# Two layer normalisations of a transformer layer, applied by ScalarE with a scale and a bias per row, in place of VectorE

## What is computed

```python
def _layernorm(x, axis=-1, eps=1e-05):
    m = jnp.mean(x, axis=axis, keepdims=True)
    v = jnp.var(x, axis=axis, keepdims=True)
    return (x - m) / jnp.sqrt(v + eps)
# attention:
q = (x @ Wq).reshape(b, n, N_HEADS, HEAD_DIM)
k, v = jnp.split(ctx @ Wkv, 2, axis=-1)
q = apply_axial_rope(q, pos_map)
k = apply_axial_rope(k, ctx_pos_map)
logits = jnp.einsum('bqhd,bkhd->bhqk', q, k) * scale
w = jax.nn.softmax(logits, axis=-1)
attn = jnp.einsum('bhqk,bkhd->bqhd', w, v)
return attn.reshape(b, n, N_HEADS * HEAD_DIM) @ Wout + bout
# feed-forward:
xn = x * jax.lax.rsqrt(jnp.mean(x * x, axis=-1, keepdims=True) + eps) * norm_w
logits = jnp.einsum('btd,gd->btg', xn, Wc) / jnp.clip(temperature, 0.1)
top_vals, top_idx = jax.lax.top_k(logits, N_ACTIVE)
expr_w = jax.nn.softmax(top_vals, axis=-1)
expressed = jnp.einsum('btk,btkc->btc', expr_w, genes[top_idx])
down = jnp.tanh(jnp.einsum('btc,dc->btd', expressed, Wd))
up = jnp.einsum('btc,dc->btd', expressed, Wu)
return down * xn * up * scale
# layer:
x = x + attention(_layernorm(x), ctx_1024, fside_BxSx2_0, fside_BxSx2_0, ...)
x = x + feed_forward(_layernorm(x), ...)
```

## Time and profile before

| | |
|---|---|
| three timed runs | 526.91, 529.20, 530.35 us; median 529.20 us |
| profiled execution, first to last instruction | 527.0 us |
| PE busy | 457.6 us, 87% of the span |
| DVE busy | 416.1 us, 79% |
| ACT busy | 258.1 us, 49% |
| POOL busy | 262.2 us, 50% |

### The profile page before, as it was taken

One profiled execution on the slowest core, in us unless ns is written; L12 is line 12 of the kernel. 1 busy time (PEld: TensorE's weight loads), 2 busy tenths in 40 slices (PEclk: granted clock), 3 DMA queues, 4 the chain that ended last, 5 costly groups with the idle time before them and its releaser, 6 DMA issues. The chain is left out here.

```text
span 527.0 us, 10932 instructions
## 1 busy us (share of the span) xinstructions
PE 457.6 (87%) x3866; PEld 336.8 (64%) x3866; DVE 416.1 (79%) x644; ACT 258.1 (49%) x386; POOL 262.2 (50%) x263
## 2 busy tenths in 40 slices
PE   1727698999999999999999999999999999796734
PEld 0525465677776767676777777777677776565523
DVE  3574274989898989899998989898989897866680
ACT  2641626374737374645555463647464737243111
POOL 0453527282919292928374655647382919110111
PEclk9967699999999999999999999999999999979776
DMA  7940504141322314050505050505041321200000
GB/s 266 283 90 18 95 1 89 25 87 26 69 64 51 84 30 103 21 109 21 109 21 109 21 109 21 109 9 113 9 92 38 73 59 37 65 23 1 21 20 21
DMA packets 81754, 34.45 MB, mean 65 GB/s; under 512 B 73136, under 2 KB 75200, under 8 KB 81728
## 3 DMA queue, kind: packets, MB, share of 16 engines
q1 hardware_dynamic: 80768, 33.05, 27.1%
q10 hardware_dynamic: 960, 1.05, 0.6%
HBM read 12.86 MB, written 4.19 MB: 32 GB/s over the span
## 5 line engine op out<-in xcount | busy, mean ns | idle before, releaser
L830 DVE MAX8 top<-stage_b 128x8 f32<-128x1024 f32 x64 | 78.0, 1218 | 32.3 <-ACT stage_b L579 32.1
L396 POOL TENSOR_TENSOR rstd<-var,minus_half 128x1 f32<-128x1 f32 x16 | 8.8, 550 | 178.1 <-DVE var L804 178.1
L838 DVE MATCH_REPLACE8 stage_b<-top,stage_b 128x1024 f32<-128x1024 f32 x64 | 77.3, 1208 | 0.0
L367 POOL TENSOR_TENSOR stage_b<-stage_b,cos_t 128x512 f32<-128x512 f32 x32 | 41.2, 1288 | 37.0 <-issue 25.5
L994 PE MATMUL gene<-wcT_h,yT_h 128*128 128x512 f32 x128 | 53.9, 421 | 1.1 <-DVE yT_l L817 1.1
L994 PE MATMUL gene<-wcT_l,yT_h 128*128 128x512 f32 x128 | 51.8, 405 | 0.0
L994 PE MATMUL gene<-wcT_h,yT_l 128*128 128x512 f32 x128 | 51.6, 403 | 0.0
L1101 PE MATMUL dense<-stage_a,v_ext 128*32 128x128 f32 x1024 | 42.6, 287 | 2.8 <-ACT stage_a L552 2.1
L536 ACT ACTIVATE parts<-turned 128x1024 f16<-128x1024 f32 x32 | 33.8, 1057 | 19.1 <-POOL turned L380 19.1
L765 DVE TENSOR_REDUCE row_max<-score_a 128x8 f32<-128x1024 f32 x32 | 38.9, 1217 | 4.8 <-PE score_a L1060 4.8
L765 DVE TENSOR_REDUCE row_max<-score_b 128x8 f32<-128x1024 f32 x32 | 38.9, 1215 | 3.7 <-PE score_b L1060 3.5
(11 more groups left out here) (149 smaller groups left out, 1129.2 us busy)
## 6 DMA issues: line engine op xcount, KB each, us to landing
x_ring<-x_dram SPq DMA_DIRECT2D x16, 256.0 KB, 2.6
out_dram<-x_ring SPq DMA_DIRECT2D x16, 256.0 KB, 2.5
ctx_sb<-ctx_dram SPq DMA_DIRECT2D x16, 128.0 KB, 2.5
stage_a<-L_ffn_Wc_dram SPq DMA_DIRECT2D x1, 2048.0 KB, 10.1
stage_b<-L_xattn_Wq_dram ACTq DMA_DIRECT2D x1, 1024.0 KB, 5.9
stage_b<-L_xattn_Wkv_dram SPq DMA_DIRECT2D x1, 1024.0 KB, 9.3
stage_b<-L_xattn_Wout_dram SPq DMA_DIRECT2D x1, 1024.0 KB, 12.5
genes_sb<-L_ffn_genes_dram SPq DMA_DIRECT2D x2, 256.0 KB, 5.2
```

Of the source, the lines that this page charges most:

```text
L367: pool.tensor_tensor(halves(qk_cos), halves(qk_sb), trig(cos_t, t), ALU.mult).then_inc(s_cosm[n], 1)
L830: nc.vector.max(top[:, 8 * n:8 * n + 8], logit if n == 0 else rest).then_inc(s_top[n], 1)
L838: nc.vector.match_replace(rest, top[:, 8 * n:8 * n + 8], logit if n == 0 else rest, REMOVED).then_inc(s_rem[n], 1)
```

## The change

The two big VectorE instructions `norm1_apply` and `norm2_apply` become ScalarE activations with the function Identity, which compute x * scale + bias with a scale and a bias per row. The scale is `rstd`; the bias is -mean * rstd, for which VectorE gets a small 128x1 instruction at the old place (`norm1_shift`, `norm2_shift`). So each normalisation now passes from GpSimd to VectorE to ScalarE. On ScalarE the first stands behind `attn_hi` and ahead of `read_v`, the second behind `ctx_hi` and ahead of `y_hi`. `ln1` on GpSimd gets a wait, because `rstd1` is now read by ScalarE. The streams of PE and SP are the same as before. The diff without its empty lines, the new semaphores and the declarations of `shift1` and `shift2`:

```diff
@@ gpsimd
             def ln1(t):
                 pool.wait_ge(s_var1, t + 1)
+                if not first(t):
+                    pool.wait_ge(s_xn, t)
                 pool.tensor_tensor(rstd1[:], var1[:], minus_half[:], ALU.pow).then_inc(s_rstd1, 1)
@@ scalar
+            act.wait_ge(s_x, 16)
+            act.wait_ge(s_shift1, 1)
+            nc.scalar.activation(xn[:], slot(0), ACT.Identity, bias=shift1[:], scale=rstd1[:]).then_inc(s_xn, 1)
             act.wait_ge(s_wkv, 16)
...
+            def norm1_apply(t):
+                act.wait_ge(s_x, (t + 1) * 16)
+                act.wait_ge(s_shift1, t + 1)
+                if not first(t):
+                    act.wait_ge(s_xT, t)
+                nc.scalar.activation(xn[:], slot(t), ACT.Identity, bias=shift1[:], scale=rstd1[:]).then_inc(s_xn, 1)
+            def norm2_apply(t):
+                act.wait_ge(s_x1, t + 1)
+                act.wait_ge(s_shift2, t + 1)
+                if not first(t):
+                    act.wait_ge(s_yT, t)
+                    act.wait_ge(s_kept, t)
+                nc.scalar.activation(yn[:], slot(t), ACT.Identity, bias=shift2[:], scale=rstd2[:]).then_inc(s_yn, 1)
...
                 if t2 is not None:
                     attn_hi(t2)
+                if later(t0, 1):
+                    norm1_apply(t0)
                 if later(t1):
                     read_v(t1)
...
                     read_q(t0)
                     ctx_hi(t0)
                 if t2 is not None:
+                    norm2_apply(t2)
                     y_hi(t2)
...
             wcT_hi(3)
+            norm1_apply(1)
             duT_hi()
@@ vector
-            def norm1_apply(t):
+            def norm1_shift(t):
                 dve.wait_ge(s_rstd1, t + 1)
                 if not first(t):
-                    dve.wait_ge(s_xT, t)
-                nc.vector.tensor_scalar(xn[:], slot(t), mv1[:, 0:1], rstd1[:], ALU.subtract,
-                                        ALU.mult).then_inc(s_xn, 1)
+                    dve.wait_ge(s_xn, t)
+                nc.vector.scalar_tensor_tensor(shift1[:], mv1[:, 0:1], -1.0, rstd1[:], ALU.mult,
+                                               ALU.mult).then_inc(s_shift1, 1)
-            def norm2_apply(t):
+            def norm2_shift(t):
                 dve.wait_ge(s_norm2, t + 1)
                 if not first(t):
-                    dve.wait_ge(s_yT, t)
-                    dve.wait_ge(s_kept, t)
-                nc.vector.tensor_scalar(yn[:], slot(t), mv2[:, 0:1], rstd2[:], ALU.subtract,
-                                        ALU.mult).then_inc(s_yn, 1)
+                    dve.wait_ge(s_yn, t)
+                nc.vector.scalar_tensor_tensor(shift2[:], mv2[:, 0:1], -1.0, rstd2[:], ALU.mult,
+                                               ALU.mult).then_inc(s_shift2, 1)
...
                 if t3 is not None:
-                    norm2_apply(t3)
+                    norm2_shift(t3)
...
                 if later(t0, 1):
-                    norm1_apply(t0)
+                    norm1_shift(t0)
```

More of the change, by code:

```diff
@@ L117, in build @@
         mv1, mv2 = sb("mv1", [P, 2]), sb("mv2", [P, 2])
-        var1, rstd1 = sb("var1", [P, 1]), sb("rstd1", [P, 1])
-        var2, rstd2 = sb("var2", [P, 1]), sb("rstd2", [P, 1])
+        var1, rstd1, shift1 = sb("var1", [P, 1]), sb("rstd1", [P, 1]), sb("shift1", [P, 1])
+        var2, rstd2, shift2 = sb("var2", [P, 1]), sb("rstd2", [P, 1]), sb("shift2", [P, 1])
         top = sb("top", [P, TOP])
@@ L148, in build @@
             "bn1_done", "mv1_done", "var1_done", "rstd1_done", "xn_done"))
+        s_shift1, s_shift2 = sem("shift1_done"), sem("shift2_done")
         s_xT, s_cT = sem("xT_in_psum"), sem("cT_in_psum")
@@ L871, in _ @@
             norm1_stats(0)
-            norm1_apply(0)
+            norm1_shift(0)
             dve.wait_ge(s_wkv_h, 1)
@@ L949, in _ @@
             scale_up()
-            norm1_apply(1)
+            norm1_shift(1)
             wcT_lo(1)
```

## The result

The changed kernel takes 540.63 us in the median of four runs (540.2 to 541.2), the kernel before in the same comparison 528.06 us (526.04 to 530.35). The ratio is 1.0232 with a 95% interval of 1.0197 to 1.0266: slower by 12.6 us. The profiled execution took 540.2 us with a span of 538.3 us. The prediction said 545.8 us (538 to 552) and slower with a chance of 0.85.

A forecast was written before the change was run, and what follows sets the result against it. The prediction took PE to bound the kernel: 14 tiles x 1.22 us of `transpose_y` delay, less 0.5 us at the last tile, gives +16.6 us, 545.8 us on the 529.2 us median; range 538 to 552 us.

The forecast's parts named there:

- What bounds the kernel: In a middle tile PE is busy 27.18 of 27.64 us; whatever makes PE wait lengthens the tile, relieving another engine hardly shortens it.
- The rival in which VectorE sets the period: VectorE holds the loop; each of 14 tiles gives back 1.96 us, 27 us in all: 502 us; chance 0.09.
- the one with the clock: The new wait drops PE's granted clock, costing 3.25 us in each of 14 tiles: 591 us; chance 0.05.
- The delay of `transpose_y`: On PE, `transpose_y` starts 1.22 us later per tile, since `yn` waits behind `ctx_hi` on ScalarE; bounds 1.05 and 1.34 us.
- I take nothing off: From `transpose_y` to `scoresT`, PE's chain and the row-max transfer both move back by the full 1.22 us.
- The delay is absorbed: Rival: PE catches up before `scoresT` because its transfer wait is looser than it looks; within 1% of 529.2 us; chance 0.06.
- the bounds of the prediction's sum: Low and high per-tile delays over 14 tiles, less 0.5 us: +14.2 us (543.4) and +19.7 us (548.9).
- what was added toward the absorbed case: The 541 to 550 us range widened a little, as part of the delay may be given back: 538 to 552 us.
- The last tile: At the end, 0.15 us on DVE, 0.06 us handover and 0.77 us on ScalarE replace 1.48 us: 0.5 us less.
- The first normalisation: On ScalarE between `attn_hi` and `read_v`, covered by a 0.81 us wait for PE: costs nothing, allowing 0 to 0.1 us per tile.
- VectorE's relief: DVE's busy time falls by some 30 us, each shift taking about 0.15 us; worth nothing in time.

The follow-up runs named there:

- experiment 4: Changed kernel with both shifts computed by tensor_scalar (a pointer and a constant) instead of scalar_tensor_tensor: 538.37 us against 529.31 us, ratio 1.0173.
- experiment 7: Changed kernel with second normalisation ahead of `read_q` and `ctx_hi`, shifts as tensor_scalar, second shift ahead of `group_max(t2, 2)`: 529.54 us against 529.16 us, ratio 1.0011.
- experiment 8: Changed kernel with only the first normalisation on ScalarE, its shift as tensor_scalar, the second back on VectorE: 528.37 us against 529.16 us, ratio 0.9997.
- Experiment 2: Changed kernel with only the second normalisation on ScalarE, behind `ctx_hi`, the first back on VectorE: 541.50 us against 529.31 us, ratio 1.0221.
- Experiment 6: Changed kernel with second normalisation between `read_q` and `ctx_hi` on ScalarE, shifts as tensor_scalar: 533.12 us against 529.16 us, ratio 1.0077.
- experiment 9: Kernel before, with only `read_q` moved behind `ctx_hi` on ScalarE, both normalisations on VectorE: 541.97 us against 529.17 us, ratio 1.0245.
- experiment 1: Changed kernel with only the first normalisation on ScalarE, the second back on VectorE: 527.33 us against 529.31 us, ratio 0.9981.
- experiment 3: Changed kernel with second normalisation moved ahead of `read_q` and `ctx_hi` on ScalarE: 543.96 us against 529.31 us, ratio 1.0288.
- experiment 5: Changed kernel with second normalisation ahead of `read_q` and `ctx_hi` on ScalarE, and both shifts as tensor_scalar: 533.46 us against 529.16 us, ratio 1.0090.

## Why the prediction was right, and where it was off

**What bounds the kernel: right.** PE is the engine whose waits count, and relief for VectorE was worth nothing (experiment 4, with 18 us less work for VectorE than after; experiments 7 and 8, with 22 and 12 us less than before). The rival in which VectorE sets the period falls with them, and the one with the clock by the 1.00 in the tile's stretch.

**The delay of `transpose_y`: right in cause and nearly in size.** The prediction had 1.22 us from an activation behind `ctx_hi`, with 0.26 us from start to start and 774 ns of its own. Measured: 0.28 us, 0.81 us and a delay of 1.29 us in the mean of nine tiles. The Trainium skill ("ScalarE: Activation LUTs", What ACT_TABLE_LOAD costs), from which the prediction worked out an estimate of 799 ns, was nearer to the 0.81 us than the value that it took from rows. Experiment 2 shows that this place carries the whole loss, and experiment 7 that it is the place and not the engine.

**"I take nothing off": this step failed.** Of 1.29 us per tile PE gives back 0.37, so that the period grows by 0.92 us. By the table: 0.26 us up to `transpose_max` and 0.30 us up to `project_k` are given back, since `transpose_max` had waited for `group_max(3)` of VectorE before (the 1.21 us from 295.47 in the earlier trace rows end at 296.68, `transpose_max` starts at 296.83 in the earlier trace rows) and `project_k` for `ctx_lo` behind it in VectorE's stream (296.60 + 0.41 = 297.01, `project_k` starts at 297.15). Now `group_max(3)` ends no later than before (VectorE starts it at 300.38, 0.12 us behind `transpose_ctx`, against 0.22 us in the rows of before), and both of PE's steps find it done. The profile names no releaser for PE's wait ahead of `transpose_max` ("issue"); that it was `group_max(3)` is read from the times. The chain of waits has it 15 times before and once after, with PE's wait for the transfer of the row maxima below it, first before, then after:

```profile
PEld score_a L1067 <- issue: 9.1, 15, 1.2
PEld score_b L1078 <- DMA qT<-neg_maxT: 6.5, 10, 2.6
```

```profile
PEld score_a L1072 <- issue: 1.2, 1, 1.2
```

The prediction had looked for slack only between `y_hi` and `y_lo`. There is none there, but there is some at the end of that chain, between `neg_max_lo` and the transfer that follows it. VectorE's and SP's timelines before:

```profile
296.60 0.41 DVE L753 TENSOR_TENSOR cT_l<-dense,cT_h 128x256 fp32r<-128x256 f32 x1
...
298.73 0.27 DVE L771 SCALAR_TENSOR_TENSOR neg_maxT<-score_a,neg_maxT 32x128 f16<-32x128 f32 x1
```

```profile
297.54 0.55 SPq L307 DMA_DIRECT2D qT<-neg_maxT  x1
298.82 0.37 SPq L259 DMA_DIRECT2D x_ring<-x_dram  x1
299.31 0.55 SPq L307 DMA_DIRECT2D qT<-neg_maxT  x1
```

After:

```profile
305.02 0.27 DVE L777 SCALAR_TENSOR_TENSOR neg_maxT<-score_a,neg_maxT 32x128 f16<-32x128 f32 x1
```

```profile
303.53 0.55 SPq L288 DMA_DIRECT2D qT<-neg_maxT  x1
304.82 0.37 SPq L240 DMA_DIRECT2D x_ring<-x_dram  x1
305.31 0.55 SPq L288 DMA_DIRECT2D qT<-neg_maxT  x1
```

Before, `neg_max_lo` ends at 299.00 and the second transfer starts 0.31 us later, behind the load of the next x in SP's stream; after, the two are 0.02 us apart (305.29 and 305.31). The second transfer starts 1.77 or 1.78 us behind the first in both, and the first follows `neg_max_hi`, which reads what `transpose_max` wrote. So, counted from `transpose_ctx`, `neg_max_lo` is 1.28 us later than before, but the transfer only 0.99 us. In experiment 9 `neg_max_lo` is 0.20 us later than before, in the mean of the nine tiles, and the transfer is not.

PE gains 0.56 us up to `project_k`, more than the transfer does, and so 0.35 us go again at `scoresT`, where PE waits for that transfer: 11.3 us in 15 waits, against 6.5 us in 10. The remaining 0.16 us are given back behind `scoresT`, 0.09 of them in the stretch to the genes; by what was not traced. Experiment 6 has the same slack: of 0.79 us it gives back 0.42. To this extent the rival "The delay is absorbed" was right, and so was its reason, a wait for the transfer that is looser than it looks.

With the measured sizes the sum is 14 x (1.29 - 0.37) = 12.9 us, against 12.6 us by the medians; the prediction had 16.6 us. That the two agree so well is in part luck, since three of the 14 tiles lost only 0.50 to 0.67 us. The 540.63 us lie below the bounds of the prediction's sum (543.4 to 548.9 us), and below the 541 us to which the spread of the timed runs widened them; only what was added toward the absorbed case reaches down to them. Some 1.1 us of the distance come from the base, which the prediction took as 529.2 us and which is 528.06 us in the comparison.

**The last tile: not borne out.** The 0.5 us off for the last tile needed a shift of 0.15 us. It took 1.21 us there:

```profile
496.49 1.21 DVE L817 SCALAR_TENSOR_TENSOR shift<-mv,rstd 128x1 f32<-128x1 f32 x1 [0.66 <-POOL rstd L379]
```

Then 1.21 us, 0.06 us to hand over and the activation's 0.81 us take the place of the 1.48 us of the earlier trace rows, a loss of 0.6 us and no gain. PE bears it out: `transpose_y` of the last tile starts 2.16 us behind the start of the shift (at 498.65), where it started 1.53 us behind that of the normalisation (at 488.37). It can't be read from the spans: what lies behind the last `ctx_hi` differs between 91.64 and 96.26 us over the profiled kernels.

**The first normalisation: right.** ScalarE's timeline after:

```profile
319.23 0.60 ACT L552 ACTIVATE aT_h<-dense 128x512 fp32r<-128x512 f32 x1 [0.16 <-PE dense L1121]
319.73 0.80 ACT L559 ACTIVATE xn<-x_ring,shift,rstd 128x512 f32 x1
320.63 0.60 ACT L515 ACTIVATE v_ext<-score_b 128x512 f32<-128x512 f32 x1
```

It fills the gap of the earlier trace rows ahead of `read_v`, ends at 320.53, and PE's transposes of `xn` start at 320.86 without a wait for it. Experiments 1 and 8 put its price at nothing.

**VectorE's relief: mis-sized, without effect on the time.** Some 30 us less were expected, 6.4 us less came, chiefly because the two shifts were priced at 0.15 us by the earlier trace rows and take five times as long; with the cheap form (experiment 4) it was 24.5 us less. In the loop the shift still ends ahead of the activation's slot (299.46 + 0.83 = 300.29, slot at 301.02), so its cost shows only once the activation is moved forward, as between experiments 3 and 5.

**Not foreseen: the second chain.** The prediction looked for slack in PE's and VectorE's streams. That `read_q` heads a chain of GpSimd with no slack either had no part in this change, since `read_q` kept its place; it decided which repairs worked.

## What to carry to other kernels

Before an instruction is moved to an engine with a low busy share, look at what stands ahead of it in that engine's stream at the moment it is needed: 0.81 us cost 0.92 us per tile behind `ctx_hi` and nothing in a gap 1.5 us earlier. When a delay is to be priced, ask for every consumer down the line what it was waiting for before; a consumer that waited for something else gives part of the delay back. And a repair that moves work forward must keep the heads of all other chains in that stream where they are.

## What the runs showed of the hardware that was not expected

**A 128x1 VectorE instruction that ends only with GpSimd's instruction beside it.** The shifts as scalar_tensor_tensor with two tensors from SBUF, by groups of line and shape of the profile after (count, busy us, mean ns), with another 128x1 instruction for comparison:

```profile
L754 DVE SCALAR_TENSOR_TENSOR shift<-mv,rstd 128x1 f32<-128x1 f32 x16 | 12.6, 786 | 5.3 <-POOL rstd L333 5.3
L817 DVE SCALAR_TENSOR_TENSOR shift<-mv,rstd 128x1 f32<-128x1 f32 x16 | 12.3, 769 | 0.7 <-POOL rstd L379 0.7
...
L810 DVE TENSOR_SCALAR var<-mv 128x1 f32<-128x1 f32 x16 | 2.5, 154 | 0.6
```

The shift at the start, with GpSimd idle, and one in the loop, on VectorE's timeline; then what GpSimd does at that place in the loop:

```profile
72.55 0.15 DVE L817 SCALAR_TENSOR_TENSOR shift<-mv,rstd 128x1 f32<-128x1 f32 x1
...
299.46 0.83 DVE L817 SCALAR_TENSOR_TENSOR shift<-mv,rstd 128x1 f32<-128x1 f32 x1
300.38 1.22 DVE L771 TENSOR_REDUCE row_max<-score_b 128x8 f32<-128x1024 f32 x1
```

```profile
298.99 1.28 POOL L393 TENSOR_TENSOR down<-down,kept 128x512 f32<-128x512 f32 x1
```

GpSimd's instruction began earlier and ends at 300.27, the shift at 300.29. In the nine tiles of the table all 18 shifts end 0.01 or 0.02 us behind a GpSimd instruction. With one tensor and a pointer instead (experiment 4) the shift takes 0.20 us at the same place, beside the same instruction of GpSimd:

```profile
300.01 0.20 DVE L817 TENSOR_SCALAR shift<-mv,rstd 128x1 f32<-128x1 f32 x1
```

```profile
299.54 1.28 POOL L393 TENSOR_TENSOR down<-down,kept 128x512 f32<-128x512 f32 x1
```

The Trainium skill ("SBUF — State Buffer", Who interferes with whom) says that a VectorE instruction with two inputs in SBUF contends with a GpSimd instruction that reads SBUF, that the order of issue decides who blocks, and that one with at most one such input, outside the modes that use two ports, does not contend. These rows agree: 0.83 against 0.20 us.

**The clock at the start of the loop.** The granted clock around 65 us was 0.59 in one profile and 1.00 in another, and the first `ctx_hi` of the middle moved by up to 3.9 us over the eleven profiled kernels: it starts between 73.55 and 75.34 where the clock from 64 to 66 us was 1.00 (six kernels), between 75.14 and 77.41 where it was 0.50 to 0.62 (five). That the clock moves it is not shown, since the rest of the start differs too. What tips it was not tried.
